# Output gate by ScalarE's Silu and the convolution's running sum in PSUM, in the second layer's sequence stage of a two-layer graph and state-space network

## The reference, cut to what matters

```python
h = jax.nn.relu(adj @ x @ gcn_w + gcn_b)
h = layer_norm(h) * ln_g + ln_b
xz = h @ w_in                                   # 4096 x 1024
xc, z = xz[:, :512], xz[:, 512:]
xpad = jnp.pad(xc, ((3, 0), (0, 0)))
xconv = sum(xpad[k:k + L] * conv_w[:, k] for k in range(4)) + conv_b
u = silu(xconv)
dbc = u @ w_xp                                  # 16 of dt, 16 of B, 16 of C
dt = softplus(dbc[:, :16] @ w_dt + b_dt)
# for each of 16 states n: h = exp(dt * A[:, n]) * h + dt * B[n] * u ; ys += h * C[n]
y = (ys + u * D_skip) * silu(z)
return y @ w_out
```

## Time and profile before

| | |
|---|---|
| Runs | 2549.86, 2549.93, 2556.5 us |
| Profiled execution | 2553.42 us, span 2551.6 us |
| Mean granted TensorE clock | 0.959 of 2.4 GHz |
| First `pre_b` | about 1110 to 1178 us |
| Scan, 512 steps | 1180 to 2319 us |
| Last gates, output and norm | 2325 to 2348 us |
| Experts | 2353 us to the end |

### The profile page before, as it was taken

One profiled execution on the slowest core, in us unless ns is written; L12 is line 12 of the kernel. 1 busy time (PEld: TensorE's weight loads), 2 busy tenths in 40 slices (PEclk: granted clock), 3 DMA queues, 4 the chain that ended last, 5 costly groups with the idle time before them and its releaser, 6 DMA issues.

```text
span 2551.6 us, 26153 instructions
## 1 busy us (share of the span) xinstructions
PE 2284.6 (90%) x8964; PEld 1420.2 (56%) x8964; DVE 2021.9 (79%) x2224; ACT 1474.1 (58%) x2192; POOL 1198.9 (47%) x906
## 2 busy tenths in 40 slices
PE   7998999999999999988989888988998886675998
PEld 4444555545555545546666565665666563343886
DVE  5666878787877866325999999999999999997765
ACT  4676666576767553225655746565674656563444
POOL 2102231314141322305878778787887878793100
PEclk9999999999999999999989999899999998598999
DMA  5232222222222231133223232322323220112121
GB/s 214 90 98 91 66 91 87 86 75 83 88 83 86 74 124 40 51 101 124 92 83 116 75 123 76 106 92 83 116 81 118 75 91 33 42 50 79 62 67 49
DMA packets 111445, 221.15 MB, mean 87 GB/s; under 512 B 7586, under 2 KB 65186, under 8 KB 110930
## 3 DMA queue, kind: packets, MB, share of 16 engines
q1 hardware_dynamic: 107106, 204.00, 24.7%
q0 software_dynamic: 3664, 14.45, 1.5%
q10 hardware_dynamic: 544, 1.05, 0.1%
HBM read 199.28 MB, written 20.19 MB: 86 GB/s over the span
## 4 chain that ended last, share of the span: by engine, by line
PE 42%; DVE 24%; POOL 12%; issue 12%; ACT 9%; DMA 0%; DVEq 0%; POOLq 0%; ACTq 0%; SPq 0%
PE ps L628 9%; POOL dB L2216 7%; DVE h L1428 5%; PE ps L670 4%; DVE wgt L1106 4%; DVE wgt L1099 3%; PE ps L920 3%; DVE acc L1402 2%; PE ps L797 2%; ACT ps L1615 2%; POOL acc L2199 2%; ACT th L1615 2%; PE ps L652 2%; POOL du L2212 2%; PE ps L732 2%
## 5 line engine op out<-in xcount | busy, mean ns | idle before, releaser
L2216 POOL TENSOR_TENSOR dB<-du,bc 128x512 f32<-128x512 f32 x512 | 673.1, 1332 | 124.8 <-DVE h L1428 119.2
L1428 DVE TENSOR_TENSOR_SCAN h<-ps,hst,dB 128x512 f32<-128x512 f32 x512 | 643.4, 1271 | 48.4 <-ACT ps L1615 36.7
L628 PE MATMUL ps<-wgt,msg 128*128 128x512 f32 x1024 | 498.1, 595 | 15.1 <-DVE wgt L1106 13.6
L1615 ACT ACTIVATE ps<-dt,cols 128x512 f32<-128x512 f32 x512 | 350.9, 687 | 272.4 <-DVE h L1428 268.8
L920 PE MATMUL ps<-consts,h 128*128 128x128 f32 x2048 | 342.9, 295 | 152.3 <-DVE acc L1402 91.2
L670 PE MATMUL ps<-raw,msg 128*128 128x256 f32 x1792 | 468.9, 397 | 0.9 <-ACT hb L1615 0.9
L920 PEld LDWEIGHTS ps<-consts,h 128*128 128x128 f32 x2048 | 258.6, 150 | 335.4 <-DVE acc L1402 153.6
L670 PEld LDWEIGHTS ps<-raw,msg 128*128 128x128 f32 x1792 | 337.2, 200 | 85.8 <-issue 49.9
L628 PEld LDWEIGHTS ps<-wgt,msg 128*128 128x128 f32 x1024 | 186.6, 190 | 219.4 <-issue 191.7
L1615 ACT ACTIVATE wgt<-wgt 128x1024 f32<-128x1024 f32 x256 | 258.4, 1049 | 56.2 <-DVE wgt L1099 54.6
L2199 POOL TENSOR_TENSOR acc<-acc,part 128x512 f32<-128x512 f32 x160 | 219.4, 1371 | 87.8 <-ACT part L1615 84.1
(11 more groups left out here) (321 smaller groups left out, 3563.4 us busy)
## 6 DMA issues: line engine op xcount, KB each, us to landing
raw<-in_adjT SPq DMA_DIRECT2D x256, 512.0 KB, 3.6
bc<-tmp_bc SPq DMA_DIRECT2D x64, 512.0 KB, 4.9
xb<-in_xT POOLq DMA_DIRECT2D x8, 512.0 KB, 4.1
tmp_x<-xb POOLq DMA_DIRECT2D x8, 512.0 KB, 3.1
x<-tmp_x SPq DMA_DIRECT2D x8, 512.0 KB, 5.4
tmp_x<-x SPq DMA_DIRECT2D x8, 512.0 KB, 4.1
raw<-tmp_xn SPq DMA_DIRECT2D x8, 512.0 KB, 4.1
tmp_xn<-x SPq DMA_DIRECT2D x7, 512.0 KB, 3.6
```

What stands on the lines that cost most here:

```text
L628: x = e.matmul(P[d][:, :], msg[:, j, d * 128:(d + 1) * 128], wgt[g % NW][:, l, :], start=j == 0, stop=j == NJ - 1)
L1428: e.tensor_tensor_scan(hr[n % 3][:, m, :], PS[4 + k % 2].t[:, :], dBr[k % 4][:, :], hst[:, n % 16, m:m + 1], ALU.mult, ALU.add).then_inc(S ...
L1615: return e.activation(out, in_, func, bias=bias, scale=scale)
L2216: e.tensor_tensor(dBr[k % 4][:, :], du[:, m, :], bcr[i % 3][:, n % 2, :], ALU.mult).then_inc(S("dB"), 1)
```

## The change

In the sequence stage of the second layer:

- The halving of w1's second half, its semaphore, and the tanh and multiply that made the gate in `pre_b` are gone. Instead ScalarE applies Silu to sz in place, in two instructions of 1024 columns, in the scan's step 6 of the next block (`gate`), under a table set of its own.
- `gates` on VectorE does its four additions first and then its four multiplies; each multiply waits for the Silu of its half.
- ScalarE writes b * w[3] + bias back into b's own PSUM bank, after the copy to xcb is complete. VectorE's first two taps write that bank, and the third writes u. The bank is free after the third tap.
- The slots are moved: NPB is 73, and tiles 0 and 2 have two more empty ones.

```diff
-        NP, NPA, NSA, NPB, NPO = 64, 55, 62, 69, 18
+        NP, NPA, NSA, NPB, NPO = 64, 55, 62, 73, 18
...
-        pre_load = mean_var + [0, 0, 0] + ([1, 1, 0, 1, 1, 0] * 2 + [0] * 4) * 2 + [0, 2, 2, 0] + [1, 0, 1, 0, 0, 0, 0, 0, 0, 0] * 2 + [0, 0]
+        pre_load = mean_var + [0, 0, 0] + ([1, 1, 0, 1, 1, 0] + [0] * 2 + [1, 1, 0, 1, 1, 0] + [0] * 4) * 2 + [0, 2, 2, 0] + [1, 0, 1, 0, 0, 0, 0, 0, 0, 0] * 2 + [0, 0]
...
 # TensorE, pre_b
-                w.wait_ge(S("w1h"), 1)
+                w.wait_ge(S("d_w1"), 16)
...
-                    if m % 2:
-                        yield from (None, None, None, None)
+                    yield from [None] * (4 if m % 2 else 2)
...
 # VectorE, start of the stage
-            w.wait_ge(S("d_w1"), 16)
             for sem, value in over_a:
                 w.wait_ge(sem, value)
-            e.tensor_scalar(w1[:, :, 512:1024], w1[:, :, 512:1024], 0.5, None, ALU.mult).then_inc(S("w1h"), 1)
...
 # VectorE, pre_b
                     w.wait_ge(S("xcb"), 4 * ib + m + 1)
-                    w.wait_ge(b.evac, b.n)
+                    w.wait_ge(S("tap"), 4 * ib + m + 1)
                     for k in range(3):
                         w.wait_ge(S("conv1"), at + k)
-                        e.scalar_tensor_tensor(c, xcb[:, m, k:k + TB], col("cw1", 4 * m + k), c, ALU.mult,
-                                               ALU.add).then_inc(S("conv1"), 1)
+                        out, signal = (b.ps[:, :], S("conv1")) if k < 2 else (u[p][:, m, :], b.evac)
+                        e.scalar_tensor_tensor(out, xcb[:, m, k:k + TB], col("cw1", 4 * m + k), b.ps[:, :], ALU.mult,
+                                               ALU.add).then_inc(signal, 1)
                         yield
-                    if m % 2:
-                        for what in (u[p][:, m - 1:m + 1, :], sz[p][:, m - 1:m + 1, :]):
...
+                    if m % 2 == 0:
+                        yield from [None] * 2
+                    else:
+                        what = u[p][:, m - 1:m + 1, :]
+                        yield
+                        n_th += 1
+                        w.wait_ge(S("tanh1"), n_th)
+                        e.scalar_tensor_tensor(what, th1[:, :, :], 1.0, what, ALU.add, ALU.mult).then_inc(S("th1r"), 1)
+                        yield from (None, None, None)
...
 # VectorE, gates
                         e.scalar_tensor_tensor(u[p][:, m, :], u[p][:, m, :], col("D1", m), b.ps[:, :], ALU.mult,
                                                ALU.add).then_inc(b.evac, 1)
+                    for m in range(4):
+                        b = gate_use(ib, m)
                         w.wait_ge(b.evac, b.n)
+                        w.wait_ge(S("silu"), 2 * ib + m // 2 + 1)
                         e.tensor_tensor(u[p][:, m, :], u[p][:, m, :], sz[p][:, m, :], ALU.mult).then_inc(S("gate"), 1)
...
 # ScalarE, pre_b
                     act(xcb[:, m, 3:TB + 3], b.ps[:, :], ACT.Identity).then_inc(S("xcb"), 1)
-                    act(u[p][:, m, :], b.ps[:, :], ACT.Identity, scale=col("cw1", 4 * m + 3), bias=col("cb1", m)).then_inc(b.evac, 1)
+                    w.wait_ge(S("xcb"), 4 * ib + m + 1)
+                    act(b.ps[:, :], b.ps[:, :], ACT.Identity, scale=col("cw1", 4 * m + 3), bias=col("cb1", m)).then_inc(S("tap"), 1)
...
                         act(th1[:, :, :], u[p][:, m - 1:m + 1, :], ACT.Tanh).then_inc(S("tanh1"), 1)
                         yield from (None, None)
-                        w.wait_ge(z.evac, z.n)
-                        w.wait_ge(S("th1r"), n_th + 1)
-                        act(th1[:, :, :], sz[p][:, m - 1:m + 1, :], ACT.Tanh).then_inc(S("tanh1"), 1)
...
 # ScalarE, scan
+                def gate(ib):
+                    for k in range(2):
+                        z = preb_use(ib, 5 + 4 * k)
+                        w.wait_ge(z.evac, z.n)
+                        what = sz[ib % 2][:, 2 * k:2 * k + 2, :]
+                        act(what, what, ACT.Silu).then_inc(S("silu"), 1)
+
                 exp(0)
                 for k in range(64 * NB + LAG):
...
-                    yield
+                    if k >= 64 + 6 and k % 64 == 6:
+                        gate(k // 64 - 1)
+                    yield
+                if 6 >= LAG:
+                    gate(NB - 1)
```

More of the change, by code:

```diff
@@ L24 @@
 TANH = "exp_and_others"
+SILU = "silu_and_others"
 GELU = "gelu_and_others"
@@ L865, in pre_b @@
                     yield from (None, None)
[L866 to L867 removed]
+                    yield from [None] * (4 if m % 2 else 2)
                 yield
                 b = preb_use(ib, 10)
[L870 removed]
+                w.wait_ge(S("th1r"), 4 * ib + 2)
                 w.wait_ge(S("d_wxd"), 32)
@@ L1327, in pre_b @@
                 yield from [None] * 5
-                n_th = 6 * ib
+                n_th = 4 * ib
                 for m in range(4):
-                    b, c, at = preb_use(ib, 2 + 2 * m), u[p][:, m, :], 12 * ib + 3 * m
+                    b, at = preb_use(ib, 2 + 2 * m), 8 * ib + 2 * m
                     yield from (None, None, None)
                     w.wait_ge(S("xcb"), 4 * ib + m + 1)
-                    w.wait_ge(b.evac, b.n)
+                    w.wait_ge(S("tap"), 4 * ib + m + 1)
                     for k in range(3):
                         w.wait_ge(S("conv1"), at + k)
-                        e.scalar_tensor_tensor(c, xcb[:, m, k:k + TB], col("cw1", 4 * m + k), c, ALU.mult,
-                                               ALU.add).then_inc(S("conv1"), 1)
+                        out, signal = (b.ps[:, :], S("conv1")) if k < 2 else (u[p][:, m, :], b.evac)
+                        e.scalar_tensor_tensor(out, xcb[:, m, k:k + TB], col("cw1", 4 * m + k), b.ps[:, :], ALU.mult,
+                                               ALU.add).then_inc(signal, 1)
                         yield
-                    if m % 2:
-                        for what in (u[p][:, m - 1:m + 1, :], sz[p][:, m - 1:m + 1, :]):
-                            yield
[L1342 to L1346, removed]
+                    if m % 2 == 0:
[7 more added lines that the diff above has]
+                        yield from (None, None, None)
                 yield from (None, None, None)
@@ L1607, in act @@
             def act(out, in_, func, scale=1.0, bias=0.0, accum=None):
-                need = {ACT.Ln: LNEXP, ACT.Exp: LNEXP, ACT.Tanh: TANH, ACT.Gelu: GELU}.get(func)
+                need = {ACT.Ln: LNEXP, ACT.Exp: LNEXP, ACT.Tanh: TANH, ACT.Silu: SILU, ACT.Gelu: GELU}.get(func)
                 if func == ACT.Exp and table[0] == TANH:
@@ L1856, in pre_b @@
                     yield
-                    if m % 2:
+                    if m % 2 == 0:
+                        yield from [None] * 2
+                    else:
                         yield
-                        w.wait_ge(S("conv1"), 12 * ib + 3 * m + 3)
+                        for x in (preb_use(ib, 2 * m), b):
+                            w.wait_ge(x.evac, x.n)
                         w.wait_ge(S("th1r"), n_th)
@@ L1922, in exp @@
                     p, at = ib % 2, 16 * m + n
-                    w.wait_ge(S("th1r"), 6 * ib + 6)
+                    w.wait_ge(S("th1r"), 4 * ib + 4)
                     w.wait_ge(S("A1"), 1)
```

4 lines of the change are left out of this document (1 added, 3 removed).

## The result

The changed kernel takes 2484.57 us (median of 4 runs, 2483.12 to 2485.07); beside it on the same chip the kernel before took 2553.12 (2549.86 to 2556.5). The ratio is 0.973, 95% interval 0.9712 to 0.9749: 68.5 us faster. The forecast was 2500 with a range from 2472 to 2534. The direction held, and the main mechanisms did.

A forecast was written before the change was run, and what follows sets the result against it. VectorE, 94% busy, was taken to bound the scan stage. Convolution stretches -45.5, gates -3.7, head -5 and tail +2.8 gave -51.4 us: 2502 from the profiled execution, 2498.5 on the median, stated as 2500, range 2472 to 2534.

The forecast's parts named there:

- What binds: Second layer's sequence stage, 1180 to 2319 us: VectorE is the bound, busy 94%, against TensorE's 85%.
- Taps: Convolution taps with the sum in PSUM fall from 1.318 to 0.73 us, removing 7.1 us of VectorE time a block.
- Density of the stretch: Convolution stretch: VectorE loses 9.7 of 43.3 us, but the 44 us stretch becomes 37.5, saving 6.5 a block, 45.5 over 7.
- The first rival: All of VectorE's time comes back: 9.5 us a block, gates 3.7, head 8.5, less 2.8; 2477 us, chance 0.13.
- The held bank: TensorE's next projection into the bank waits for the third tap: zero to 1 us a tile, inside the 37.5.
- ScalarE's second write: ScalarE's write to PSUM waits for its first, 28 pairs: a few tenths each on an engine 40% idle, counted as nothing.
- Silu at the block's end: Two table loads and two Silu, a 4.6 us burst per block, hidden by 3.6 us of cover; uncovered up to 32 us.
- Gates' order: At a block's end, multiplies grouped behind four additions avoid GpSimd: 28 x (0.824 - 0.692) = 3.7 us saved.
- Head: Before the first scan: without w1's halving the subtraction comes 4.7 us earlier, clock up to 3.5 more; 5 us saved.
- Tail: After the last block: output matmuls start 1.5 us later and Ln's table load adds 1.3; 2.8 us lost.

The follow-up runs named there:

- the kernel with one tap of three: Changed kernel with only the first tap reading the sum from PSUM and writing u; the other two read xcb and u in SBUF: 2528.98 us, ratio 0.9907.
- The run with 77 slots: Changed kernel with the tail's edit, u's silu as Silu on ScalarE, and NPB 77 for 73, one more slot per tile: 2517.13 us, ratio 0.9851.
- the new tail: Changed kernel, last block only: additions and multiplies alternate, Silu made earlier, Ln's table set loaded right behind it: 2479.87 us, ratio 0.9705.

## Why the prediction was right, and where its sizes were off

- **What binds.** Right. VectorE was the bound of the stage, and taking 11.0 us a block from it shortened the block by 9.4.
- **Taps.** Right in mechanism, shown by undoing it (47 us) and by the kernel with one tap of three. 0.749 us was measured where 0.73 was taken from L1402: a tap pays 0.02 more, 1.6 us in all. No gap between writing PSUM and writing SBUF shows: 749 against 748 ns.
- **Density of the stretch: the term that was mis-sized.** The prediction took 6.5 us a block of its 9.7, because at 1640 VectorE had been 93% busy and a held bank was feared. The stage became 9.4 a block shorter; less the 1.0 that the gates gave (below), the term measured 8.4, so 13 us more over the stage. Two causes. First, 11.0 us a block left VectorE, not 10.2 (9.7 and the gates' 0.5): u's multiply fell from 1613 to 1225 ns (0.8 a block), which the old slots take back. The prediction had read contention on the taps and on the gates' multiply, and not on this neighbour, another instruction with two SBUF inputs. Which slot freed it was not looked at. Second, TensorE ran without the reserve that it was given: 96% busy at full clock against 34.5 of 37.5. The first rival, 10.0 a block with its gates, described the stage better than the forecast with its 7.0; its 2477, with 8.5 for the head, lies 8 us under the result, and the forecast lies 15 above.
- **The held bank.** Its cost was put at zero to 1 us a tile. In the changed kernel TensorE waits there 5.3 us in eight waits. The old slots show that the fear was sound and that the two slots' lead decides.
- **ScalarE's second write: counted as nothing, and wrong.** VectorE waits 19.8 us for it, in 22 waits, 0.7 for each of 28 tiles. VectorE gave up 11.0 us a block and the stage became 9.4 shorter; the missing 1.6 a block, 11 us over seven, can lie in this wait, but no run shows how much of it does. The run with 77 slots made the wait smaller and lost more elsewhere.
- **Silu at the block's end.** Right: full cover, shown by moving the burst by two steps, which costs 33 us against the 32 that were named. Silu is ready 2.16 us before the first multiply.
- **Gates' order.** Mis-sized too: 3.7 us forecast, 7.1 measured from first addition to next scan. The contended multiply was read rightly (824 to 684 ns on average); that four additions in a row, and four multiplies, overlap more than dependent pairs do was not in the sum.
- **Head.** 5 forecast, 7.2 measured. The subtraction comes 4.7 us earlier in the head, as named; the other 2.5 come behind it, where the matmuls run at full clock. The clock did not fall, as the text allowed for with up to 3.5 us more.
- **Tail.** The sum, 2.8 against 3.0, came out by luck, from partly wrong reasons. The prediction read L904's 7.13 us as the low clock. It was the full clock, as the windows of the kernel before show (first row), and in the changed kernel the same 16 matmuls took 8.77 at a mean of 0.81 (second fence), the first of them at 1.2 GHz and the later ones at 2.4 (0.86 and then 0.43 us apart):

```profile
2328.30:2335.50 7.20, 7.13 (x16) 2.96 (x16) 4.71 (x7) 0.00 (x0) 0.00 (x0) 1.00 0.68 242
2319.00:2328.00 9.00, 7.90 (x40) 5.57 (x40) 5.13 (x8) 1.29 (x3) 0.00 (x0) 0.81 0.10 27
```

```profile
2257.30:2266.10 8.80, 8.77 (x16) 3.60 (x16) 2.46 (x4) 0.00 (x0) 0.00 (x0) 0.81 0.36 134
...
2248.00:2257.00 9.00, 6.48 (x40) 4.54 (x40) 6.78 (x11) 4.57 (x5) 0.00 (x0) 1.00 0.31 90
```

  In the 9 us ahead of the output matmuls it is the other way round (0.81 before, 1.00 after), which brought the first addition 1.7 us nearer to the last scan. So: -1.7, +1.85 for four additions ahead of the first multiply, +1.64 for L904's clock, +1.28 for the load: 3.1. The clock's two terms were not in the prediction, and they nearly cancel.

The Trainium skill ("SBUF — State Buffer", on who interferes with whom) has two SBUF inputs of VectorE contend with GpSimd's reads and one not; the taps, the gates' multiplies and u's multiply agree. The Trainium skill ("ScalarE: Activation LUTs", on what a table load costs) adds a drain of 1.38 us to a load. This trace shows none: Silu starts at 1594.56 behind a load of 1593.27 that lasts 1.28, and the exponential at 1597.88 behind the load of 1596.58.

## What to carry to other kernels

When VectorE and GpSimd both run without a break, look at each VectorE instruction that has two SBUF inputs, all of them, and compare it with one of the same size that reads PSUM; moving one operand to PSUM was worth 43% of the instruction here (1318 to 749 ns). Holding that bank longer needs slots between the uses, and they must be measured, since four fewer cost 32 us here and four more, in a sister version, 26. A burst of table loads of 4.6 us was free where VectorE had the last scan steps of a block and 5 us of gates to do, and cost its full length two scan steps later. And look at the order of short dependent pairs: four additions and then four multiplies took 1.0 us less than four pairs in turn.

## What the runs showed of the hardware

- Contending two-input instructions do not only slow down: two in a row took 3.43 us beside GpSimd's products (2.95 for two), where two with a PSUM operand take 1.5. GpSimd pays as well, 1462 ns a product before and 1335 after in the convolution.
- `scalar_tensor_tensor` with an operand in PSUM takes 724 to 753 ns on average for 512 columns in all these kernels, written to PSUM or SBUF alike, and none of these groups shows the contention.
- In the head, TensorE kept its clock over 1.54 us of idle time (two matmuls in 1.12, granted 1.00) and had lost it after 5.40 and 6.27 (2.08 and 2.07, granted 0.50). In the tail, the same idle time of 2.40 us is followed by 1.12 us with the new tail (granted 1.00) and by 2.08 in the changed kernel (granted 0.59 over the stretch). That L904 had run at full clock before it does not explain this: it had in the kernel before too, and the pair took 2.08:

```profile
2340.63 2.08 PE L568 MATMUL ps<-sq,consts 128*128 128x512 f32 x2 [2.40 <-ACT sq L1615]
```

- The same holds for L904 itself: behind the same 1.92 us of idle time it took 8.77 us in the changed kernel, and 7.13 in the one with one tap of three and in the one with Silu of u. So the 3.1 us that the clock gives back in the new tail are measured, but nothing here says how to get them on purpose.
